# A state-space layer with routing on one core: three pieces of work moved by one slot in a hand-written order

## The reference

```
# layer 1: selective scan, D = 512, E = 1024, N = 16 states
resid_norm = rmsnorm(resid) * norm_w
skip = resid_norm @ W_skip;  x_in = resid_norm @ W_in
x = silu(causal_conv4(x_in) + conv_b)
delta = softplus(x @ W_delta_1 @ W_delta_2 + b_delta_2);  Bm = x @ W_B;  Cm = x @ W_C
h[l] = h[l-1] * exp(delta[l] * A) + (delta[l] * x[l]) * Bm[l]      # for each channel and state
y[l] = sum over n of h[l] * Cm[l]
out = resid + ((y + x * W_D) * silu(skip)) @ W_out
# layer 2: router over 64 experts, softmax, top 8
out = flat * sum(top_w) + sum over k of top_w[k] * expert_bias[top_idx[k]]
```

## Time and profile before

| | us |
|---|---|
| median of 3 runs | 2380.44 |
| lowest and highest | 2377.85, 2384.84 |
| the profiled execution | 2379.91 |
| its span in the trace | 2378.0 |
| PE busy | 1958.7 (82%) |
| POOL busy | 1913.5 (80%) |
| DVE busy | 1795.4 (75%) |
| ACT busy | 1669.1 (70%) |
| mean granted TensorE clock | 0.94 of full speed |

### The profile page before, as it was taken

The page is one execution under the profiler, slowest core; times in us unless marked ns, Lnnn a source line. Parts: engine busy times, 40 slices in busy tenths (PEclk is TensorE's granted clock), DMA queues, the critical chain, the costliest instruction groups (busy, mean ns, idle before and its releaser), DMA issues. The chain is left out here.

```text
span 2378.0 us, 35550 instructions
## 1 busy us (share of the span) xinstructions
PE 1958.7 (82%) x11717; PEld 1584.2 (67%) x11717; DVE 1795.4 (75%) x3105; ACT 1669.1 (70%) x3276; POOL 1913.5 (80%) x1192
## 2 busy tenths in 40 slices
PE   5577777898889898898889898898889988797883
PEld 3456666777667676777667686776667776666551
DVE  3377877798697977888697977889697887887522
ACT  2368686877769685787779686786868687787421
POOL 1279898898789797989879897998879898999512
PEclk9988988999999999999999999999999999999996
DMA  4555556665747565674657556574757646555320
GB/s 159 169 178 182 189 177 215 201 216 157 225 151 239 180 215 183 203 229 150 210 175 235 196 186 215 185 228 148 232 169 222 194 154 207 181 183 160 120 71 18
DMA packets 239281, 434.31 MB, mean 183 GB/s; under 512 B 19134, under 2 KB 135418, under 8 KB 239098
## 3 DMA queue, kind: packets, MB, share of 16 engines
q1 hardware_dynamic: 239098, 432.04, 56.9%
HBM read 347.57 MB, written 84.41 MB: 182 GB/s over the span
## 5 line engine op out<-in xcount | busy, mean ns | idle before, releaser
L608 POOL TENSOR_TENSOR hc<-h,c_all 128x1024 f32<-128x1024 f32 x512 | 1205.0, 2365 | 219.5 <-DVE h L953 160.0
L953 DVE TENSOR_TENSOR_SCAN h<-operand,carry,bank 128x512 f32<-128x512 f32 x480 | 597.1, 1271 | 174.1 <-PE bank L1129 142.7
L1134 PE MATMUL y_sum<-ident,hc 128*128 128x128 f32 x4096 | 624.7, 281 | 13.0 <-POOL hc L608 12.7
L1129 PE MATMUL bank<-ident,u_t 128*128 128x128 f32 x2560 | 417.3, 288 | 243.2 <-DVE h L953 219.7
L722 ACT ACTIVATE u_t<-dx_t,b_t 128x256 f32<-128x256 f32 x1280 | 575.0, 499 | 0.5 <-PE bank L1129 0.5
L1129 PEld LDWEIGHTS bank<-ident,u_t 128*128 128x128 f32 x2560 | 312.4, 148 | 375.1 <-issue 240.2
L1134 PEld LDWEIGHTS y_sum<-ident,hc 128*128 128x128 f32 x4096 | 506.1, 146 | 79.8 <-issue 50.2
L592 POOL TENSOR_TENSOR operand<-dx_q,b_all 128x1024 f32<-128x1024 f32 x192 | 454.5, 2367 | 11.0 <-DMA b_all<-bc_dram 11.0
L703 ACT ACTIVATE bank<-delta_q,neg_a 128x512 f32<-128x512 f32 x384 | 262.5, 684 | 263.1 <-DVE h L953 262.7
L703 ACT ACTIVATE operand<-delta_q,neg_a 128x512 f32<-128x512 f32 x640 | 432.9, 714 | 0.0
L953 DVE TENSOR_TENSOR_SCAN h<-bank,carry,operand 128x512 f32<-128x512 f32 x288 | 354.9, 1270 | 33.1 <-POOL operand L592 16.4
(11 more groups left out here) (124 smaller groups left out, 2009.3 us busy)
## 6 DMA issues: line engine op xcount, KB each, us to landing
c_all<-bc_dram SPq DMA_DIRECT2D x256, 512.0 KB, 4.3
b_all<-bc_dram SPq DMA_DIRECT2D x192, 256.0 KB, 5.2
win<-in_L_attn_W_in SPq DMA_DIRECT2D x64, 512.0 KB, 5.7
wskip<-in_L_attn_W_skip SPq DMA_DIRECT2D x64, 512.0 KB, 6.2
x_dram<-x SPq DMA_DIRECT2D x64, 256.0 KB, 4.5
delta_dram<-delta SPq DMA_DIRECT2D x32, 512.0 KB, 7.3
dx_dram<-dx SPq DMA_DIRECT2D x32, 512.0 KB, 7.3
delta_q<-delta_dram SPq DMA_DIRECT2D x32, 512.0 KB, 5.8
```

The lines of the kernel that those rows point to most:

```text
L608: nc.gpsimd.tensor_tensor(hc[:, number % 3], h[:, number % 3], c_all[:, j % 2, s % 2:s % 2 + 1].to_broadcast([P, 2, SPAN]), ALU.mult).then ...
L953: nc.vector.tensor_tensor_scan(h[:, number % 3, q], first, second, start, ALU.mult, ALU.add).then_inc(scan_done.sem, 1)
L1129: last = transpose(bank[:, q, b * P:(b + 1) * P], u_t[:, j % 2, b, q * P:(q + 1) * P], ident[:])
L1134: return matmul(to, lhsT=of, rhs=ident[:], is_transpose=True, start=start, stop=stop, skip_group_check=True)
```

## The change

Three placements are shifted by one slot; no instruction is added, removed or altered.

- PE: pair 0's in-projection goes from s = -2 late and -1 early to s = -3 late and -2 early, that is from slots 30 and 31 to slots 29 and 30 of the step before. The other pairs stay.
- DVE: the two residual sums go from s = 30 and 43 to s = 31 and 44.
- PE: the out-projection's second half goes from s = 31 to 38 to s = 32 to 39, that is from slots 31 and 0 to 6 to slots 0 to 7. The first half stays.

```diff
@@ DVE, "mix" @@
-                                if s in (30, 43):
-                                    b = s // 43
+                                if s in (31, 44):
+                                    b = s // 44
@@ PE, "prep" @@
-                                if (s, late) in ((3 * p - 2, 1), (3 * p - 1, 0)):
-                                    e = s - 3 * p + 2
+                                first = 3 * p - 2 if p else -3
+                                if (s, late) in ((first, 1), (first + 1, 0)):
+                                    e = s - first
@@ PE, "mix" @@
-                            b = int(s >= 31)
-                            et = 2 * (s - 26) + late if not b else s - 31
-                            if 26 <= s < 30 or (31 <= s < 31 + ET and late):
+                            b = int(s >= 32)
+                            et = 2 * (s - 26) + late if not b else s - 32
+                            if 26 <= s < 30 or (32 <= s < 32 + ET and late):
```

## The result

| | before | changed |
|---|---|---|
| median, us (12 runs each) | 2379.05 | 2388.8 |
| lowest to highest | 2375.78 to 2384.84 | 2382.27 to 2393.08 |
| span of the profiled execution | 2378.0 | 2385.3 |

The ratio is 1.0038, 95% interval 1.0027 to 1.0049: slower by 9.0 us (6.4 to 11.7). The two profiled executions are not quite typical ones: 2379.91 and 2387.19 us of device time, so their difference is 7.3 and not 9.0.

The account below looks back on a forecast made before the run. The prediction took a relay of DVE, POOL and PE as the bound, with PE ending each step. Its terms, 4.3 + 2.4 + 1.9 + 1.9 + 0.6 + 0.3 - 2.6 = +8.8 us, gave 2389.2 us, range 2379 to 2397.

Parts of the forecast that it names:

- What bounds the kernel: Each step is a relay: DVE slots 0 to 11, POOL 12 to 27, PE 27 to 0; PE sets the boundary.
- rival 4: At boundaries, ACT's hv waits less for pair 0's in-projection, so faster: 2375 us; chance 0.10 together with rival 3.
- Full boundary, 0.43: At the ten boundaries into chunks 4 to 13, late scans replace the logits' stall: 0.43 us each, +4.3 us.
- an odd boundary has the same steps: A boundary behind the long DMA stall: row maximum at 643.15 against 642.73, again 0.4 us later.
- the 0.6 for chunk 3: Second sum of z in chunk 3, where POOL has no routing work and cover is thinner: +0.6 us once.
- Early boundaries, 6.2: Into chunks 1, 2 and 3, no logits' stall absorbs the delay: +1.9, +1.9 and +2.4 us.
- Rival 1: Delays into chunks 1 to 3 are taken in: +2.6, 2383 us; chance 0.24, shared with the ten boundaries at zero.
- The second sum, 0: Moved from slot 11 to 12, ahead of scan 13, it costs DVE 0.6 us, covered by busy POOL: 0.
- Into 14, +0.3: At the first boundary without preparation, into chunk 14, the sum of z delays scan 0: +0.3 us.
- without such cover: Out-projection matmul moved from slot 31 to 7: hidden, so 0; uncovered, 0.87 x 12 = 10 us either way.
- Tail, -2.6: In three tail steps, one fewer out-projection matmul stands ahead of the transposes: -0.85 us each, -2.6 us.
- Rival 3, the clock: Matmul moved into slot 7 keeps PE's clock up: 2372 us, step 3 alone -1.8; chance 0.10 together with rival 4.

Follow-up runs that it names:

- the second measurement: The changed kernel run once more, unaltered, with a second profile: ratio 1.0038 (1.0024 to 1.0052) to the kernel before.
- the sum put back: The changed kernel with the first sum of z back in slot 30: ratio 1.0026 (1.0014 to 1.0038) to the kernel before.
- the in-projection alone: The kernel before with only pair 0's in-projection one slot sooner, sums and out-projection unchanged: ratio 1.0023, +5.5 us.
- the two kernels with a sum put back: The changed kernel with the first sum of z back in slot 30, or the second in slot 11: ratios 1.0026 and 1.0031 to the kernel before.
- the out-projection late: The kernel before with the out-projection in slots 31, 0 to 6 and 8 to 11, sums of z in 7 and 12: ratio 0.9911, -21.2 us.
- ahead of dx: The kernel before with pair 0's in-projection in slots 26 and 27, ahead of PE's wait for dx: ratio 0.9901, -23.6 us.

## Why the prediction was right, and where it wasn't

Forecast 2389.2, measured 2388.8 and in the second measurement 2388.5 us, a ratio a little over the 0.3% that the prediction took for the least that can be told from no change. The single terms fit less well than their sum: the second sum of z was priced some 3 us too low, the odd steps 2.8 too high and the way into 14 by 0.9 too high. So the path and most terms were right, and that the total came out at 8.8 against 9.0 is in part luck.

**What bounds the kernel.** Held. PE sets the end of a step and nothing on it moved: the logits come 4.50 us after the second turn's new place (1051.99 - 1047.49), where the forecast had 1047.48 - 1042.94 = 4.54. From there on it is DVE's late chain that ends the boundary, 0.46 us behind the logits, as forecast. That hv's waits fell by 22.9 us (about 20 forecast) and brought nothing refutes rival 4.

**Full boundary, 0.43.** Right in size and cause: +0.4 at scan 0 in nine of the ten full steps, and 0.4 less in all ten with the sum put back. But "an odd boundary has the same steps" was only half the story: what is late when a step reaches an odd chunk's wait for dx is partly taken in there. Steps from an odd chunk cost 0.0 and -0.2 in sum, where 2.8 stood (boundaries, and the sum in chunk 3), and the steps from an even chunk +3.7 and +2.3 for 2.1. The term of 4.3, plus the 0.6 for chunk 3, came out as 3.7 and 2.1.

**Early boundaries, 6.2.** Right within the scatter: +5.3, +6.1, and +5.7 with the in-projection alone, but +8.8 and +9.1 in the two kernels with a sum put back, whose in-projection is the same. Into chunk 3 the boundary itself shows the forecast +2.4 (+3.1, +0.4, -1.1) in both traces of the changed kernel; into chunks 1 and 2 it reads 0.4 to 3.0 and 1.6 to 2.8 over the five traces, for the 1.9 forecast. Rival 1 falls: these delays are not taken in.

**The second sum, 0.** This step failed, by 0.6 in each even step. The prediction looked for cover on POOL and tied it to a wait of POOL for DVE. Slots 12 to 16 of chunk 6, POOL and PE of the changed kernel:

```profile
974.88 0.68 DVE L1059 TENSOR_TENSOR z<-mixed,z 128x512 f32<-128x512 f32 x1
...
977.50 0.63 PE L1129 MATMUL bank<-ident,u_t 128*128 128x128 f32 x4 [1.35 <-DVE h L953]
```

```profile
988.27 2.36 POOL L608 TENSOR_TENSOR hc<-h,c_all 128x1024 f32<-128x1024 f32 x1
991.02 2.37 POOL L608 TENSOR_TENSOR hc<-h,c_all 128x1024 f32<-128x1024 f32 x1 [0.40 <-PE y_sum L1134]
```

and PE's turn at the same place in the kernel before:

```profile
972.93 0.63 PE L1129 MATMUL bank<-ident,u_t 128*128 128x128 f32 x4 [0.75 <-DVE h L953]
```

The sum delays scan 13, so PE waits 1.35 us instead of 0.75 for it before it may turn u for slot 14. All that PE has queued behind that turn (the products for B and C, the skip branch, the sums of y) is 0.6 late, and POOL, which reuses the buffer that the sum of y reads, waits 0.32 to 0.40 us, ten times, where it had no wait. The delay reached POOL, but by way of PE, which the prediction had not followed. That PE carries it is read from the order of its queue; no run took it away.

**Into 14, +0.3.** Wrong in sign: -0.6 at scans 0 and 1 (+0.4 and -1.0). PE behind the logits, and scan 1, of the kernel before:

```profile
2001.17 1.12 PE L1339 MATMUL mixed<-wout,ys 128*128 128x512 f32 x2
2002.14 0.60 PE L1129 MATMUL bank<-ident,u_t 128*128 128x128 f32 x4
```

```profile
2002.87 2.45 DVE L953 TENSOR_TENSOR_SCAN h<-operand,carry,bank 128x512 f32<-128x512 f32 x2 [0.92 <-PE bank L1129]
```

Here scan 1 waited 0.92 us behind the out-projection's first matmul of slot 31, since no convolution stood ahead of it. The prediction named that price ("without such cover") and didn't ask where the cover is missing: the same -1.0 stands at the boundary into 15.

**Tail, -2.6.** The mechanism held. In the third tail step the changed kernel has three matmuls (x6) ahead of the transposes, one fewer than the earlier trace rows:

```profile
2327.82 2.84 PE L1340 MATMUL mixed<-wout,ys 128*128 128x512 f32 x6
2330.50 0.38 PE L1223 MATMUL routed<-ident,rem 128*64 128x128 f32 x2
```

2.68 us between the two starts, where it was 3.54: 0.86 each, as forecast. But only 0.7 of 2.6 was left in this execution. One of the skip branch's products took 6.72 us, where the kernel before had 3.69, at the high clock:

```profile
2291.74 3.69 PE L1315 MATMUL routed<-rnt_gate,wskip 128*128 128x256 f32 x16 [2.75 <-DVE gate L1037]
```

```profile
2297.98 6.72 PE L1316 MATMUL routed<-rnt_gate,wskip 128*128 128x256 f32 x16 [2.73 <-DVE gate L1037]
```

which is +3.03, less the 1.04 us by which its successor's wait (2.10 for weights, before) is longer than the usual 1.06: 2.0 us, and 2.6 - 2.0 is the measured rest. It is always the same product, the second of four, behind 2.7 us of idle: it took 6.74 with the in-projection alone and 5.19 to 5.38 in five other traces, and of these eight only the kernel before had it at 3.69, by luck. (The product at the same place one step earlier took 5.38 in all eight; with the out-projection late the idle ahead is 1.06 us, and none is slow.) Reckoned in the same way, the tail without this product is 2.6 to 2.7 us shorter in all five traces that have the move, and 0.0 and 0.1 shorter with the in-projection alone and ahead of dx, which don't. So the forecast -2.6 is shown.

**Rival 3, the clock.** It did not come in the full steps from chunk 4 on. Behind the idle of slots 8 to 11 the turn is as slow as in the earlier trace rows:

```profile
969.50 1.09 PE L1129 MATMUL bank<-ident,u_t 128*128 128x128 f32 x4 [5.19 <-DVE h L953]
```

One matmul in slot 7 leaves the 5.19 us of idle as they were, as the point against it said. With the out-projection's second half in slots 8 to 11 the idle is 1.23 us and the turn takes 0.63 (rows above). Windows of both (us, busy PE, PEld, DVE, ACT, POOL, mean granted clock, DMA share, GB/s), changed kernel first:

```profile
969.00:974.00 5.00, 4.50 (x22) 4.08 (x23) 3.21 (x5) 5.00 (x10) 4.95 (x3) 0.66 0.02 8
```

```profile
962.00:967.00 5.00, 4.16 (x27) 3.53 (x28) 4.02 (x5) 5.00 (x10) 4.50 (x2) 1.00 0.00 0
```

1.00 is 2.4 GHz; 0.66 is a stretch partly at 1.2. Scan 12 came 1.1 to 1.3 us sooner in each full step, and scan 13 gave 1.0 of it back, 0.6 of that for the sum of z. The Trainium skill ("TensorE: Matmul & The Clock Gate", Part 1) has activity release the throttle; the trace agrees here with these numbers. The rival was right that the turn can be kept at the high clock, wrong in the trigger, and high in the gain (1.75 forecast).

In chunk 3 the rival came true in one execution of two. The matmul in slot 7 shortens the idle there from 3.70 to 2.84 us, and in the first profile of the changed kernel the turn behind it ran at the high clock:

```profile
540.60 0.63 PE L1129 MATMUL bank<-ident,u_t 128*128 128x128 f32 x4 [2.84 <-DVE h L953]
```

Scans 2 to 12 of that step came 2.2 us sooner, where the rival had 1.8 for "step 3 alone". In the second profile the turn behind the same 2.84 us took 0.86, and nothing came sooner (+0.2). The 2.2 us stand in the first profile's column "from odd".

**What stays open.** The spans of the two profiles are 7.3 and 6.1 us longer than that of the kernel before, the runs say 9.0 with an interval from 6.4; which column the other executions differ in isn't known. Whether the start costs a microsecond or two with the in-projection moved can't be told: the same instructions scatter there by 4.1 us.

## What to carry to other kernels

In a hand-ordered stream find each engine's last long wait before the point that sets the end, and ask on which side of it a piece of work stands: moved across it, two halves of in-projection were worth 23.6 us, moved about behind it they cost 5.5. A stall can be spent once: cost two delays at one boundary together, not each against the whole stall. And follow a delay through every in-order queue behind the waiting instruction, not only to the engine that looks like the bound; then ask, for each price that cover made zero, in which steps that cover is missing.

## What the runs showed of the hardware

PE's granted clock dropped behind an idle of 5.19 us and not behind one of 1.23 in the same slots; behind 2.84 us in chunk 3 the same turn took 0.63 us in one execution and 0.86 in the next. In the tail the same 16 matmuls took 3.69 us at a granted clock of 1.00 (2.4 GHz; 2306.30 to 2309.80 of the changed kernel), 5.38 at 0.68 (part of them at 1.2 GHz; 2252.90 to 2258.20) and 6.72 at 0.54 (2298.00 to 2304.60). Which of these a product behind 2.7 us of idle got changed from one execution to the next: for effects of a few microseconds that scatter is as large as the effect.
